# A macaron block (feed-forward, selective scan, feed-forward) on one core: the down projection in fp32 from a ring of seven hidden tiles, instead of in fp16 high and low parts

## The reference

```
x = x + 0.5 * ffn(layernorm(x))
x = x + ssm(layernorm(x))
x = x + 0.5 * ffn(layernorm(x))

ffn(x):  h = silu(x @ wg.T) * (x @ wu.T);  return h @ wd.T     # hidden width 768, int weights / 127
ssm(x):  z = x @ W_z.T;  params = x @ W_params.T               # 64 + 16 + 16 columns
         dt = softplus(params[..., :64] @ W_dt.T + b_dt);  u = silu(causal_conv4(x))
         h[t+1] = exp(dt[t] * A) * h[t] + B_tilde[t] * u[t]    # 256 channels x 16 states
         y = sum over the 16 states of C * h, + u * D;  return (y * silu(z)) @ W_out.T
```

## Time and profile before

| | us |
|---|---|
| median of 3 runs | 2953.18 |
| lowest, highest | 2952.47, 2956.13 |
| the profiled execution | 2959.91 |
| its span, first to last instruction | 2958.1 |
| TensorE, busy | 2489.4 (84%) |
| VectorE, busy | 2433.1 (82%) |
| GpSimd, busy | 2162.7 (73%) |
| ScalarE, busy | 2062.7 (70%) |

### The profile page before, as it was taken

One profiled execution on the slowest core, in us unless ns is written; L12 is line 12 of the kernel. 1 busy time (PEld: TensorE's weight loads), 2 busy tenths in 40 slices (PEclk: granted clock), 3 DMA queues, 4 the chain that ended last, 5 costly groups with the idle time before them and its releaser, 6 DMA issues. The chain is left out here.

```text
span 2958.1 us, 32072 instructions
## 1 busy us (share of the span) xinstructions
PE 2489.4 (84%) x10292; PEld 1277.8 (43%) x10292; DVE 2433.1 (82%) x2588; ACT 2062.7 (70%) x2949; POOL 2162.7 (73%) x1542
## 2 busy tenths in 40 slices
PE   4768889898988989898898989889898988988676
PEld 2333444444444444444444444444444444443334
DVE  3269888989889898988989898898989888898982
ACT  2558687776868778686877868687786868767453
POOL 1358788787778878787887878778787877878672
PEclk9877899989989998998999899899989989988778
DMA  1000000000000000000000000000000000000000
GB/s 56 15 8 8 1 17 12 15 12 11 15 8 15 15 15 8 15 15 8 15 15 15 8 15 15 8 15 15 15 8 15 15 8 15 15 1 8 7 15 15
DMA packets 37545, 38.69 MB, mean 13 GB/s; under 512 B 2209, under 2 KB 37122, under 8 KB 37378
## 3 DMA queue, kind: packets, MB, share of 16 engines
q1 hardware_dynamic: 37378, 36.63, 3.8%
HBM read 19.85 MB, written 16.78 MB: 12 GB/s over the span
## 5 line engine op out<-in xcount | busy, mean ns | idle before, releaser
L796 POOL TENSOR_TENSOR acc<-acc,ring 128x1024 f32<-128x1024 f32 x512 | 1209.6, 2362 | 420.3 <-DVE ring L994 401.0
L964 DVE TENSOR_TENSOR_SCAN ring<-du_bank,ring 128x1024 f32<-128x1024 f32 x512 | 1168.1, 2282 | 5.2 <-ACT du_bank L721 5.2
L994 DVE SCALAR_TENSOR_TENSOR ring<-ring,inv_a,c_bank 128x1024 f32<-128x1024 f32 x512 | 653.5, 1276 | 245.9 <-issue 233.3
L576 PE MATMUL c_bank<-c_parts,pick 64*128 64x512 f32 x1024 | 411.5, 485 | 224.0 <-DVE ring L994 223.9
L768 POOL TENSOR_TENSOR hid_lo<-hid,hid_hi 128x512 f16<-128x512 f32 x384 | 448.2, 1168 | 147.8 <-ACT hid_hi L676 147.6
L732 ACT ACTIVATE ring<-dt,a_coef 128x1024 f32<-128x1024 f32 x512 | 546.0, 1137 | 1.2
L676 ACT ACTIVATE hid_hi<-hid 128x512 f16<-128x512 f32 x384 | 240.5, 627 | 324.6 <-DVE hid L913 280.9
L512 PE MATMUL work<-wd_t,hid_hi 128*128 128x256 f16 x1536 | 403.0, 303 | 28.2 <-POOL hid_lo L768 28.2
L512 PE MATMUL work<-wd_t,hid_lo 128*128 128x256 f16 x1536 | 398.3, 301 | 0.0
L576 PEld LDWEIGHTS c_bank<-c_parts,pick 64*128 64x128 f32 x1024 | 167.8, 204 | 480.7 <-issue 430.0
L501 PE MATMUL work<-xt_hi,wg_t 128*128 128x512 f16 x768 | 313.7, 408 | 51.0 <-ACT xt L619 18.5
(11 more groups left out here) (108 smaller groups left out, 3110.3 us busy)
## 6 DMA issues: line engine op xcount, KB each, us to landing
x_in<-L_attn_x SPq DMA_DIRECT2D x32, 512.0 KB, 3.8
out<-x_fin SPq DMA_DIRECT2D x32, 512.0 KB, 2.9
ring<-L_ffn_w_gate SPq DMA_DIRECT2D x1, 768.0 KB
ring<-L_ffn_w_up SPq DMA_DIRECT2D x1, 768.0 KB
ring<-L_ffn_w_down SPq DMA_DIRECT2D x1, 768.0 KB
ring<-L_attn_W_z SPq DMA_DIRECT2D x1, 256.0 KB
ring<-L_attn_W_out SPq DMA_DIRECT2D x1, 256.0 KB
ring<-L_attn_W_params SPq DMA_DIRECT2D x1, 96.0 KB
```

Source lines behind the costliest of these rows:

```text
L576: last = pe.matmul(c_bank[:, c * CH:(c + 1) * CH], pick[C_ROW:P, s:s + 1].to_broadcast([P - C_ROW, P]), c_parts[bt % 2][C_ROW:P, c * CH:(c ...
L796: nc.gpsimd.tensor_tensor(acc[bt % 2][:, h, :], acc[bt % 2][:, h, :], cg[:, slot, :], ALU.add).then_inc(S["summed"], 1)
L964: scan = nc.vector.tensor_tensor_scan(g[:, i, :], du_bank[:], decay[:, a, :], 0.0, ALU.add, ALU.mult)
L994: nc.vector.scalar_tensor_tensor(cg[:, k, :], g[:, i, :], inv_a[:, h, s:s + 1], c_bank[:], ALU.mult, ALU.mult).then_inc(S["weighted"], 1)
```

## The change

The split goes. `hi` and `lo` are removed with their tiles, 384 instructions on ScalarE and 384 on GpSimd; the ring `hid` grows from 3 to 7 tiles, and the down weights `wd_t` are kept in fp32. A down job now has 12 fp32 matmuls of 256 columns, reads `hid` directly and waits for the last `sh` of its chunk instead of the last `lo`. A ring tile is written again seven products later, so `sh` with m > 0 waits for the last down job of the chunk before; the wait for `lo` goes. The tables `AT`, `PACE` and `LAG` have new numbers throughout.

```
-HIDS = 3
+HIDS = 7
 AT = {
-    "gu1": [-33.77, -24.26], "dn1": [-23.9, -23.41, -16.87, -16.12],
+    "gu1": [-33.82, -24.24], "dn1": [-25.59, -23.36, -17.66, -17.06],
-    "dn2": [54.98, 55.18, 62.08, 62.25],
+    "dn2": [54.47, 54.68, 61.58, 62.54],
...
-                for kind in ("sh", "hi", "lo"):
-                    at(t + LAG["up"][0] + LAG[kind][0], kind, f, b, c, m)
+                at(t + LAG["up"][0] + LAG["sh"][0], "sh", f, b, c, m)
...
+            elif kind == "sh":
+                self.unit[ev] = len(self.unit)
+                chunks.append(ev[1:4])
+                if self.unit[ev] >= HIDS:
+                    self.was[ev] = ("dn",) + chunks[self.unit[ev] - HIDS] + (1,)
...
-        hid_hi = sb("hid_hi", [P, HM, CH], F16)
-        hid_lo = sb("hid_lo", [P, HM, CH], F16)
-        wd_t = sb("wd_t", [P, HM, E], F16)
+        wd_t = sb("wd_t", [P, HM, E])
...
                 elif kind == "dn":
-                    wait(pe, "lo", ("lo", f, bt, c, HM - 1))
+                    wait(pe, "free", ("up", f, bt, c, HM - 1))
...
-                            for i, part_ in enumerate((hid_hi, hid_lo)):
-                                last = pe.matmul(dst[:, j * E:(j + 1) * E], part_[:, m, t:t + P], wd_t[:, m, :],
-                                                 start=(m == 0 and i == 0), stop=(m == HM - 1 and i == 1))
+                            last = pe.matmul(dst[:, j * E:(j + 1) * E], hid[:, K.unit["sh", f, bt, c, m] % HIDS, t:t + P],
+                                             wd_t[:, m, :], start=(m == 0), stop=(m == HM - 1))
...
                 # VectorE, kind "sh"
-                        i = K.at["lo", ("lo",) + ev[1:]][1] % HIDS
-                        wait_before(dve, "lo", ("lo",) + ev[1:], HIDS)
+                        i = K.unit[ev] % HIDS
+                        if ev in K.was:
+                            wait(dve, "ready", K.was[ev])
```

More of the change, by code:

```diff
@@ L74 @@
 AT = {
[6 rows of a table removed]
[6 rows of a table added]
 }
 PACE = {
-    "gu1": 0.901, "gu2": 1.091,
+    "gu1": 0.892, "gu2": 1.092,
 }
 LAG = {
[6 rows of a table removed]
[6 rows of a table added]
 }
@@ L187, in __init__ @@
         self.order = schedule()
-        self.at, self.bank, self.prev, self.was = {}, {}, {}, {}
-        last, order, count = {}, {}, {}
+        self.at, self.bank, self.prev, self.was, self.unit = {}, {}, {}, {}, {}
+        last, order, count, chunks = {}, {}, {}, []
         place = {ev: i for i, ev in enumerate(self.order)}
@@ L266, in increments @@
         one = {"bc": "c_spread", "db": "du_in", "gate": "gated", "pe": "c_high", "u0": "u_first", "dt0": "dt_first", "ai": "acc_begun",
-               "d": "du", "da": "sp_exp", "dl": "sp_ln", "dp": "sp_sum", "si": "silu", "hi": "hi",
-               "lo": "lo", "lr": "rstd", "Ts": "lowered", "lx": "normed", "ex": "decay", "scan": "scanned"}
+               "d": "du", "da": "sp_exp", "dl": "sp_ln", "dp": "sp_sum", "si": "silu",
+               "lr": "rstd", "Ts": "lowered", "lx": "normed", "ex": "decay", "scan": "scanned"}
         if kind in one:
@@ L668, in _ @@
                     nc.scalar.activation(dt[bt % 2][:, :, 0:1], dt[bt % 2][:, :, 1:2], ACT.Copy).then_inc(S["dt_first"], 1)
[L669 to L676, removed]
                 elif kind == "pe":
@@ L763, in _ @@
                     nc.gpsimd.tensor_scalar(shift[:, slot, :], shift[:, slot, :], -1.0, None, ALU.mult).then_inc(S["rstd"], 1)
[L764 to L769, removed]
                 elif kind == "dp":
```

## The result

The changed kernel takes 3020.84 us, the median of 4 runs (3019.28 to 3024.04), against 2954.46 before, now of 4 runs as well; the ratio is 1.0226, 95% interval 1.0209 to 1.0244. It is slower by 2.3%, 66 us. The profiled execution took 3019.28 us, 59.4 more than the one of before.

A forecast was written before the change was run, and what follows sets the result against it. Bound: the sum of the longer of TensorE's and VectorE's work in each slot. Profiled 2959.9 us, +51 for the clock, +9 for the ends, gives 3020; median 3013 us, 2.0% slower, range 2905 to 3095.

The forecast's parts named there:

- What bounds the kernel: TensorE and VectorE in lockstep: each slot lasts as long as the longer of their work, about one slot of slack.
- The price of a job: Down job on TensorE: 2.63 us before, 5.2 after as 24 records; 8 a period, +20.5 us of TensorE work.
- The new places and the freed latencies pay for the longer jobs: Period at full clock: VectorE's gaps sum to 22.2 us against 22 to 22.6 before, so the period would not change.
- Single slots: Gaps forecast slot by slot, such as 0.7 us in 14 and 15, 2.7 in 20, 3.7 in 30 to 0.
- What is removed ... I count the busy time itself at nothing: GpSimd's 448.2 us and ScalarE's 240.5 us removed count as nothing; only 1.8 us latency ahead of a down job remains.
- The clock: Thin slots 6, 14, 22, 30: 1.7 us lost at two of four places, +3.4 us a period, +51 us in all.
- Rival 1: Faster: the clock holds and two relieved queues stop delaying TensorE; period -3 to -4 us, 2910 us; chance 0.25.
- The ends: Ahead of the first scan +6.7 us, at the end of the chain +2.7 us, together +9 us.
- the credit of 5.8 and 1.8 us for the split at the end of the chain: End of the chain: removing the split takes 5.8 and 1.8 us off the +10.3 us of longer jobs for two chunks.
- The rule of the Trainium skill: L952 on VectorE, two SBUF inputs, contends with GpSimd; removing the subtractions gives back 6 us, sum would be 3007.

The follow-up runs named there:

- e2: Kernel before, split and old order kept, each down job's 24 fp16 matmuls run twice (5.2 us a job): 3283.70 us, ratio 1.1115.
- e4: Changed kernel plus eight fp16 matmuls with overwritten result ahead of the spreading of C in slot 5: 2990.36 us, ratio 1.0122 to before.
- e1: Changed kernel with hid and down weights in fp16, each down job's 12 matmuls run twice, low part left out: 2773.10 us, ratio 0.9385 to before.
- e7: e1 with the tables AT, PACE and LAG of the kernel before: 2910.47 us, ratio 0.9867 to before.
- e8: e1 with 384 ScalarE copies and 384 GpSimd subtractions put back, nobody waiting for their results: 2804.67 us, ratio 0.9507 to before.
- e9: e1 with a ring of 13 hidden tiles instead of 7: 2771.99 us, ratio 0.9391 to before.
- e3: Changed kernel (no split, fp32 down jobs) with the tables AT, PACE and LAG of the kernel before: 3205.51 us, ratio 1.0848 to before.
- e5: Changed kernel with hid and down weights in fp16, 12 matmuls a down job run once, low part left out: 2784.51 us, ratio 0.9440 to before.
- e6: Changed kernel with hid and down weights in fp32r, 12 matmuls a down job run once: 2786.43 us, ratio 0.9442 to before.

## Why the prediction was right

The forecast was 3013 us, measured 3021, and the mechanism held: slower by the low clock in a thin slot, and by the ends. But the number is better than its parts. Against the profiled execution of before it was +60, measured +59.4: 14 periods +48 for +44.5, batch 0 +3 for -0.2, the ends +9 for +15. That these cancel is luck. By its steps:

- **What bounds the kernel**: held. A slot lasts as long as the longer of TensorE's and VectorE's part; slot 24 kept its 7.03 us to the hundredth while everything around it moved. e2 shows it from the other side: 20.5 us more work in full slots costs 19.7.
- **The price of a job**: 24 records 0.216 apart, the 5.2 us of the forecast; 5.45 with the last one's tail, against 2.79 before. The growth of 2.6 us held.
- **"The new places and the freed latencies pay for the longer jobs" at full clock**: held to about a microsecond. e4, in which the clock no longer falls in slots 5 to 8, has a period of 173.9 against 173.2. Its gaps are 23.7 us, for the 22.2 of the forecast; VectorE's busy time, forecast as unchanged, gave 0.8 back. The parts are larger than I put them. From the runs: longer jobs +15.1 (e1 to after), order -9.1 (e7 to e1), split -2.8 (before to e7), together +3.2.
- **Single slots** missed by up to 2 us both ways and cancelled. Slots 14 and 15 came out at 2.4 us for 0.7, slots 30 to 0 at 5.2 for 3.7; slots 4, 16 to 18, 20, 26 and 28 came out lower, by 3 us in all.
- **"What is removed ... I count the busy time itself at nothing"** was wrong. e8 puts it at 2.0 us a period. If it is the same in the old order, it is most of the split's 2.8; I had booked only the latency. No run took the copies out of the old order, so that stays open.
- **The clock**: 1.7 us for a job in a thin place was right (7.13 against 5.45). Two of four places was not: of 6, 14, 22 and 30 only slot 6 had more than 0.4 us of low clock in a period. It still cost 2.4 us instead of 1.7, as slot 9 came late by the low clock of slot 8. So the term was 3.4 us a period and measured 2.4. The low clock fell from 34.6 to 17.1 us a period, and most of that is the order and not the longer jobs: 37.5 in e7, 23.2 in e1 with the new order, 17.1 with the longer jobs. Slots 14 and 22 have none in e1 either. Rival 1's condition was met, the granted clock in the periods is 0.95, and the kernel was slower all the same: of the low clock that is gone, 10.3 us had lain in slots 7, 15 and 27, where VectorE had no gap before.
- **The ends**: +9 expected, +15 measured. The start was +1.9 for +6.7: the longer jobs cost 9.4 (e1 to after), the split gave 4.7 back and not 3.6 (before to e7), and the order 2.8 more (e7 to e1). The end was +13.1 for +2.7. Of it 2.6 lie in the slots of batch 15, for which I had no term, and 10.5 behind its last product. There the step that failed is the credit of 5.8 and 1.8 us for the split at the end of the chain: TensorE's waits ahead of the two pairs of down jobs fell by 3.1 us only, from 1.87 and 2.88 to 0.84 twice. Before, TensorE ran gate and up jobs while the subtractions went on, and it has the same jobs to run now. The rest is the clock: behind the last product TensorE worked for 18.8 us at the low level, for 11.8 before, and half of the 7.0 is an estimate of 3.5 us. That part no run ties to the change: e1 and e9, alike but for the ring, have 20.8 and 12.2 us there, and take 76.1 and 71.9 us from the last product to the end. The end of the chain after:

```profile
2982.25 10.63 PE work L508 x48
2992.88 8.65 PE work L498 x40
3001.53 0.04 DVEq L366
...
3001.61 0.70 DVE hid L896
...
3002.35 10.64 PE work L508 x48
```

Between the two pairs of down jobs stand now 40 gate and up matmuls, 8.65 us. Before, the chain counts 16 in 3.5 us and then 7.2 us to the next pair; but TensorE ran 36 of them, to 2945.3, and only then waited. Its timeline at the second pair, before and after:

```profile
2948.23 0.28 PE L512 MATMUL work<-wd_t,hid_hi 128*128 128x256 f16 x1 [2.88 <-POOL hid_lo L768]
...
3002.35 10.63 PE L508 MATMUL work<-wd_t,hid 128*128 128x256 f32 x48 [0.84 <-DVE hid L896]
```

- **The rule of the Trainium skill** ("SBUF — State Buffer", "Who interferes with whom"): L952, now L935, fell further than by the estimate of 6 us.

```profile
L935 DVE SCALAR_TENSOR_TENSOR acc<-u,d_skip,acc 128x512 f32<-128x512 f32 x64 | 59.3, 926 | 2.3
```

That is 13.5 us less than in the earlier trace rows, but only 1.8 of it comes without the subtractions in the old order (e3, 71.0 us). The traces show beside what the 64 instructions ran. With nothing on GpSimd beside them they took 0.75 us (2 of them before, 16 after). Beside GpSimd's sums into `dt`, two SBUF tiles added into one, they took 1.24 us on average (47 before) and 1.32 (18 after). The 14 that met a subtraction before took 0.87, 1.7 us more in all than alone. So the gain of the subtractions is 1.7 us and not 6; the rest is that fewer meet the sums into `dt`, by the order and by the longer jobs (e1 has 69.3 us in the same order). The trace agrees with the rule, and the estimate failed in sharing the 30 us out by busy time.

## What to carry to other kernels

Where two engines hand one buffer to and fro, as here, busy totals of 84% and 82% are not slack: list the work of both between two handovers, and price a change by the places where the longer engine gets longer. Work that is moved or lengthened should go where the other engine is the longer one; without the split, the same 20.5 us cost 18.1 a period in the old order (e7 to e3) and 15.1 in the new. And a latency taken out of a chain's end is no gain if the engine behind it used the wait for work that it still has to do.

## What the runs showed of the hardware

- A shorter job can make the kernel slower through the clock. Down jobs of 1.3 us gave 2785 us, of 2.6 us 2773, with 30 and 23 us of low clock in a period; the gap of slot 24 follows the low clock in it: 5.3 us with none, 6.6 to 7.0 with 3.4 us of it, 8.1 with 6.8. Eight matmuls that nobody reads, ahead of a job in a thin place, took 30 us off the whole. For the clock as such the Trainium skill, "TensorE: Matmul & The Clock Gate", "The HAM clock gate", says that activity releases the throttle; the traces of e4 and e5 agree.
- fp32r matmuls of 128x256 follow each other at 0.120 us, while the load of their weights is recorded at 0.188 us each. So the record of the load is no bound for the pace, as I had taken it to be for e6; true fp32 is at 0.216 for each of two records, fp16 at 0.109.
- One VectorE instruction of 128x512 fp32 with two SBUF inputs took 0.75 us alone and 1.2 to 1.3 us on average beside a GpSimd sum of two SBUF tiles.
